# Identity products ahead of TensorE's waits in the last batch of a decoder layer's attention

## The reference

```
x = layernorm(x + ssm(x))                       # in_proj, causal conv, silu, selective scan
                                                #   (512 channels, 16 states, chunks of 64), gate, out_proj
x = layernorm(x + attention(x, ctx, ctx))       # 16 heads of 16, scores / 4, softmax, times v, w_o
x = layernorm(x + experts(x))                   # 8 experts by position, silu(x w1) * (x w3) w2, width 704
```

```
scores = einsum('bhqd,bhkd->bhqk', q, k) / sqrt(16)
attn   = softmax(scores, axis=-1)
out    = einsum('bhqk,bhkd->bhqd', attn, v)     # then heads side by side, times w_o, plus b_o
```

## Time and profile before

| | us |
|---|---|
| median of three runs | 2745.58 (2741.46 to 2746.72) |
| the profiled execution | 2741.8 |
| its span, first to last instruction | 2740.0 |
| TensorE (PE) busy | 2429.5 (89%) |
| VectorE (DVE) busy | 2123.5 (77%) |
| GpSimd (POOL) busy | 2073.6 (76%) |
| ScalarE (ACT) busy | 1821.1 (66%) |

### The profile page before, as it was taken

The page is one execution under the profiler, slowest core; times in us unless marked ns, Lnnn a source line. Parts: engine busy times, 40 slices in busy tenths (PEclk is TensorE's granted clock), DMA queues, the critical chain, the costliest instruction groups (busy, mean ns, idle before and its releaser), DMA issues. The chain is left out here.

```text
span 2740.0 us, 49530 instructions
## 1 busy us (share of the span) xinstructions
PE 2429.5 (89%) x14854; PEld 1667.0 (61%) x14854; DVE 2123.5 (77%) x3232; ACT 1821.1 (66%) x3972; POOL 2073.6 (76%) x999
## 2 busy tenths in 40 slices
PE   6678898989898898889999989988997879999997
PEld 5456666666666666666666666666665545555554
DVE  3788999999999999999999999999999722222333
ACT  3667888888888888888888887888887531111111
POOL 5999999999999999999999999999999400000000
PEclk9888999999999999999999999999998869999999
DMA  5355666666666666666666666666665342432221
GB/s 154 112 152 147 168 168 161 160 167 170 175 161 168 171 171 163 163 165 167 165 165 176 160 177 162 171 163 160 160 160 156 101 118 65 119 120 80 80 80 31
DMA packets 270168, 399.66 MB, mean 146 GB/s; under 512 B 115441, under 2 KB 190449, under 8 KB 265810
## 3 DMA queue, kind: packets, MB, share of 16 engines
q1 hardware_dynamic: 254546, 384.95, 52.9%
q10 hardware_dynamic: 15360, 11.55, 1.6%
HBM read 300.89 MB, written 94.37 MB: 144 GB/s over the span
## 5 line engine op out<-in xcount | busy, mean ns | idle before, releaser
L519 POOL TENSOR_TENSOR arena<-arena 128x1024 f32<-128x1024 f32 x512 | 1207.6, 2364 | 33.6 <-DMA arena<-w_dram 33.3
L623 ACT ACTIVATE dA_ps<-arena,a_neg 128x256 f32<-128x256 f32 x2048 | 880.1, 465 | 256.3 <-DVE arena L800 125.7
L800 DVE TENSOR_TENSOR_SCAN arena<-dA_ps,arena 128x512 f32<-128x512 f32 x672 | 802.7, 1207 | 75.5 <-ACT dA_ps L623 52.2
L529 POOL TENSOR_TENSOR arena<-arena 128x1024 f32<-128x1024 f32 (+1 forms) x416 | 808.4, 1943 | 18.0 <-DVE arena L800 15.0
L800 DVE TENSOR_TENSOR_SCAN dA_ps<-dA_ps,arena 128x512 f32<-128x512 f32 x352 | 415.7, 1204 | 3.8 <-POOL arena L519 3.4
L920 PE MATMUL a_ps<-xT,w_conv 128*128 128x256 f32 x1536 | 367.3, 389 | 0.0
L863 DVE TENSOR_REDUCE mx<-s_ps 128x2 f32<-128x512 f32 x497 | 333.4, 671 | 18.6 <-PE s_ps L920 18.6
L920 PEld LDWEIGHTS a_ps<-xT,w_conv 128*128 128x128 f32 x1536 | 286.5, 193 | 53.9 <-issue 16.3
L679 ACT ACTIVATE probs<-st_ps 128x512 f32<-128x512 f32 x493 | 285.2, 578 | 27.6 <-PE st_ps L920 25.4
L920 PE MATMUL s_ps<-k_st,q_st 96*128 96x256 f32 x994 | 262.2, 346 | 38.8 <-DVE mx L863 29.3
L920 PE MATMUL y_ps<-arena,sel 128*32 128x256 f32 x4096 | 258.5, 395 | 37.5 <-POOL arena L529 33.9
(11 more groups left out here) (117 smaller groups left out, 3275.4 us busy)
## 6 DMA issues: line engine op xcount, KB each, us to landing
arena<-delta_dram SPq DMA_DIRECT2D x512, 128.0 KB, 2.9
arena<-w_dram SPq DMA_DIRECT2D x512, 128.0 KB, 3.3
arena<-bc_dram SPq DMA_DIRECT2D x128, 256.0 KB, 4.5
q_st<-q_parts_dram SPq DMA_DIRECT2D x512, 64.0 KB
k_st<-k_parts_dram SPq DMA_DIRECT2D x512, 64.0 KB
w_dram<-u SPq DMA_DIRECT2D x32, 512.0 KB, 3.1
delta_dram<-delta SPq DMA_DIRECT2D x32, 512.0 KB, 3.9
k_parts_dram<-parts SPq DMA_DIRECT2D x32, 512.0 KB, 4.2
```

Source lines behind the costliest of these rows:

```text
L519: pool.tensor_tensor(dBu[:, n % NB], w_r[:, n // RP % 2, t % RP].unsqueeze(1).to_broadcast([P, QS, L]), bc_r[:, b.par, 0], ALU.mult).then_ ...
L529: pool.tensor_tensor(h[:, n % NH, states], h[:, n % NH, states], bc_r[:, b.par, 1, states], ALU.mult).then_inc(s_hC, 1)
L623: last = nc.scalar.activation(dA[n % NDA][:, q], delta_r[:, n // (2 * RP) % 2, t % RP], ACT.Exp, scale=a_neg[:, t, 2 * half + q:2 * half + ...
L800: nc.vector.tensor_tensor_scan(dst, decays, dBu[:, n % NB, 2 * half:2 * half + 2].rearrange("p q t -> p (q t)"), 0.0, ALU.mult, ALU.add).t ...
```

## The change

A helper `drain_products` issues `count` products ident x ident (128x128, f32) into a PSUM bank that is free at that point, and nothing for any batch but the last. It is called ahead of the waits in the pieces of the attention, and as pieces of their own (`idle`) before and behind transposes at the end. In `scores` and `scores_T` the wait for the stack and the wait for the rows of maxima move from the head of the piece to behind the products, so behind the wait for the bank; that holds for all batches. There are 158 products in all. The results are never read.

```diff
--- before.py
+++ after.py
@@ -923,6 +923,15 @@
                 for _ in range(count):
                     mm(s_ps[:, 0], g[:, 0, 0:P], g[:, 0], True, True)
 
+            def drain_products(b, count, out=None):
+                if b.c < B - 1:
+                    return
+                if out is None:
+                    bank_y.wait_read(pe)
+                    out = y_ps[:, 0:P]
+                for _ in range(count):
+                    mm(out, ident[:], ident[:], True, True)
+
             pe.wait_ge(s_zero, 1)
             idle_products(16)
             pe.wait_ge(s_const_v, N_BIAS)
@@ -1046,6 +1055,11 @@
                     bank_f.read_by(s_v, 1, b, 1)
                 return piece
 
+            def idle(count):
+                def piece(b):
+                    drain_products(b, count)
+                return piece
+
             def x_of(b):
                 return xt[:, b.c % NX]
 
@@ -1079,7 +1093,6 @@
             def scores(hd):
 
                 def piece(b):
-                    pe.wait_ge(s_stack[hd // HG], b.value(STACK_DMAS * 16, STACK_DMAS * 16))
                     n = b.value(H, hd)
                     if n:
                         pe.wait_ge(s_max, n - 1 if n > LATE_S + 1 else n)
@@ -1088,6 +1101,8 @@
                         for half in range(2):
                             pe.wait_ge(s_scan[half], NU * B)
                     out = scores_bank(n)
+                    drain_products(b, {0: 11}.get(hd, 0), out[:, 0, 0:P])
+                    pe.wait_ge(s_stack[hd // HG], b.value(STACK_DMAS * 16, STACK_DMAS * 16))
                     for tt in range(TT):
                         i = mm(out[:, tt], q_st[:, hd, tt * P:(tt + 1) * P], k_st[:, hd], True, True)
                     i.then_inc(s_s_mm, 1)
@@ -1095,6 +1110,7 @@
 
             def max_transpose(gr):
                 def piece(b):
+                    drain_products(b, 4 if gr < 2 else 0)
                     pe.wait_ge(s_max, b.value(H, HG * gr + HG))
                     bank_y.wait_read(pe)
                     nc.tensor.transpose(y_ps[0:HG * TT, L:],
@@ -1106,7 +1122,6 @@
             def scores_T(hd):
 
                 def piece(b):
-                    pe.wait_ge(s_m_row, b.value(NG * 16, 16 * (hd // HG) + 16))
                     n = b.value(H, hd)
                     if n:
                         pe.wait_ge(s_exp, n - 1 if n > LATE_ST + 1 else n)
@@ -1115,6 +1130,8 @@
                         for half in range(2):
                             pe.wait_ge(s_scan[half], NU * B)
                     out = scores_T_bank(n)
+                    drain_products(b, {4: 6, 8: 6, 12: 12}.get(hd, 0), out[:, 0, 0:P])
+                    pe.wait_ge(s_m_row, b.value(NG * 16, 16 * (hd // HG) + 16))
                     for kt in range(TT):
                         i = mm(out[:, kt], k_st[:, hd, kt * P:(kt + 1) * P], q_st[:, hd], True, True)
                     i.then_inc(s_st_mm, 1)
@@ -1123,6 +1140,7 @@
             def pv(gr):
 
                 def piece(b):
+                    drain_products(b, 5 if gr >= NG - 2 else 0)
                     pe.wait_ge(s_exp, b.value(H, HG * gr + HG))
                     pe.wait_ge(s_v, b.value(1, 1))
                     bank_f.wait_read(pe)
@@ -1137,6 +1155,9 @@
 
             def head_transpose(gr):
                 def piece(b):
+                    drain_products(b, (4, 22, 4, 5)[gr])
+                    if gr == 1 and b.c == B - 2:
+                        drain_products(b.ahead(1), 11)
                     pe.wait_ge(s_oT, b.value(NG, gr + 1))
                     bank_f.wait_read(pe)
                     for tt in range(TT):
@@ -1148,6 +1169,7 @@
 
             def attn_out(tt):
                 def piece(b):
+                    drain_products(b, 5 if tt == 0 else 0)
                     pe.wait_ge(s_onT, b.value(1, 1))
                     if tt == 0:
                         bank_a.wait_read(pe)
@@ -1172,9 +1194,12 @@
                 *[(O_OF, attn_out(tt)) for tt in range(TT)],
                 *[(O_OUT, out_proj(tt)) for tt in range(TT)],
                 *[(O_K, k_proj(m)) for m in range(KD)],
+                (O_ONT - 2, idle(4)),
                 (O_ONT - 2, transpose(lambda b: on, s_on, NG, s_onT_mm, s_onT, bank_a, a_ps)),
                 *[(O_Q, q_proj(m)) for m in range(KD)],
+                (O_X2T, idle(34)),
                 (O_X2T, transpose(x_of, s_x2, TT, s_x2T_mm, s_x2T, bank_a, a_ps)),
+                (O_X2T, idle(16)),
                 *[(O_ON + HG * gr, head_transpose(gr)) for gr in range(NG)],
                 (O_XP, x_proj),
                 *[(O_MT + HG * gr, max_transpose(gr)) for gr in range(NG)],
```

## The result

The changed kernel takes 2754.91 us (median of five runs, 2752.64 to 2758.85) against 2745.58 (median of five, 2741.46 to 2747.37): 1.0045 times as long, 95% interval 1.0033 to 1.0057. I had forecast 2746.5 us, within 0.2% of before; it is slower by more than that. The profiled execution takes 2757.5 us, span 2755.7, so 15.7 us more than the one of before. Between the means of the five runs it is 11.0 us: the profiled execution of before was a quick one, that of the changed kernel a slow one.

The account below looks back on a forecast made before the run. TensorE's gaps in the drain, and the low clock behind them, bound the kernel. A full clock gives 10.4 us, the products' overshoot takes it back: +2.6 us on a mean of 2743.9 makes 2746.5 us, range 2737 to 2757.

Parts of the forecast that it names:

- The mark: Experts' start: a warm first g_ps at 2259.4 us would equal the cold one at 2257.47, which loses 1.95 us.
- The page's dips: Granted clock on the profile page before: full nearly everywhere, dips in slices 32 and 33, the drain of the attention.
- The price of a product: TensorE, one f32 product of 128 columns: 0.24 us, range 0.21 to 0.32, from halving rows of 256 columns.
- The cheap rival: A product costs near the transposes' 0.07 to 0.13 us, so the whole 10.4 us is gained: 2733.5 us; chance 0.18.
- the dear one: Rival: 128-column streams do not hide their weight load, a product costs 0.32 us, +12.4 us: 2756.3 us; chance 0.20.
- The last 122 products and the work between: Drain from 2216.1 us to g_ps: 29.3 us of products plus work and waits, g_ps at 2262.0, +2.6 us.
- the cover: Products standing on TensorE's late waits, longer than these: 8.2 us on 4.25, 8.2 on 3.1 + 1.63, 3.8 on 2.67.
- The first 36 products: 2192 to 2216 us: later stack loads are won back by groups running warm, 0 us, range -1.5 to +1.5.
- The two waits stand in another order before the same matmul, which goes with the later one: 0: Moved waits in scores and scores_T, every earlier batch: the order of the waits changes nothing, 0 us.
- The clock: Sign: granted clock 1.00 from 2192 us through the experts' start; 0.50 anywhere in the stretch would show the forecast wrong.
- Slower by over 0.2%: Outcome for the whole kernel, slower by more than about 5.5 us: chance 0.27, against 0.52 same and 0.21 faster.

Follow-up runs that it names:

- e3: Changed kernel with 78 products instead of 158, both waits as before up to batch 30, no wait where a count is 0: 0.9972 of before, -7.9 us.
- e10: The kernel of e3 again, on another chip: 0.9982 of before, -4.5 us.
- e8: e3's 78 products, with both waits moved in all batches: 0.9994 of before, -1.0 us.
- e2: Changed kernel with its 158 products, but both waits as before up to batch 30: 1.0032 of before, +7.9 us.
- e4: e2 without the last 34 and 16 products: 1.0018 of before, +5.0 us.
- e1: Kernel before with only both waits moved in all batches, no products: 1.0026 of before, +6.8 us.
- e9: The kernel of e1 again, on another chip: 1.0021 of before, +6.7 us.
- e5: Kernel before with only the wait for the stack in scores moved, no products: 0.9996 of before, 0.0 us.
- e12: Kernel before with only the wait for the rows of maxima in scores_T moved, no products: 1.0015 of before, +5.6 us.

## Why the prediction was wrong, step by step

- **The mark** (start of g_ps plus 1.95 us for its cold start) was right: from the first g_ps on, the changed kernel needs 1.8 us less. The page's dips are slices 31 to 33, not 32 and 33.
- **The price of a product**, 0.24, was near: 0.223 in the longest group and 0.24 in those of five, and 122 of them 27.6 us instead of 29.3. The cheap rival (0.07 to 0.13) falls, and so does the dear one at 0.32: halving the two rows, 0.23 and 0.24, was the right way to a price that no row showed. The Trainium skill's rule (TensorE: Matmul & The Clock Gate, section Back-to-back issue gap) would have made it an estimate of 0.29. The trace disagrees: 0.223 / 2 = 0.11 an instruction is what half the columns of the earlier trace rows give, with no more for the load.
- **The last 122 products and the work between** were put at 16.65 + 29.3 = 45.95 us and took 45.2. The sum is closer than its parts: the products took 1.7 less, the work and waits between them 17.6, 0.95 more. That the cover is longer than the waits was right; e3, e10 and e8 show it from the other side.
- **The first 36 products** were put at 0, -1.5 to +1.5, and the stretch took 3.6 us more. It is again what stands above the waits: with 21 products in it, e3 goes from its max transpose at 2195.88 to 2219.32 in 23.4 us, as before (23.6), while e2, e4 and the changed kernel, with 36, take 27.2 to 27.4. It is not the first eleven: the first scores come 3.1 us behind the max transpose where it was 1.9, but behind the products TensorE still waits 0.36 us for the stack, and e1 and e9, without a product, have 3.1 and 3.0. (In e2 and e4 no wait is left behind the eleven; there it is 2.5.) At the heads' transpose the products stand above the wait; then TensorE waits for DMAs all the same: 0.97 us for the stack of head 8, 1.47 and 1.24 for the rows of heads 0 and 4, the last behind its six products. The groups between did not win it back. Which of the 36 products moved these DMAs no run shows. It is a term sized too small, by 3.6.
- **"The two waits stand in another order before the same matmul, which goes with the later one: 0"** is the step that failed. It was the one edit that works in all 32 batches, and it costs 6.7 +- 2.4 us (e9; 6.8 +- 2.6 in e1), about half of the loss. What I reasoned about, when this matmul may start, is not what costs: the pair of matmuls ends no later behind what it waits for (last section). What the runs show in its place is that ScalarE, VectorE and GpSimd wait longer in the batches, GpSimd by 6.5 us in all between the means of the table. How the order of two waits brings that about stays open.
- **The clock**: forecast 1.00 throughout, with 0.50 anywhere as a sign of being wrong; it was 0.50 for 6 us at 2220, behind waits of 0.97 and 1.47 us that have no products ahead of them. From 2228 us on it was right.
- In sum: +2.6 was forecast for the drain and +5.5 came, of which 3.6 are the first stretch; 0 for all else and about +6.7 came. Slower by over 0.2% had 0.27.

## What to carry to other kernels

Filler ahead of a wait must be shorter than the wait, counted at its own measured price: what it overshoots goes on the path, while what it falls short costs nothing as long as the clock stays up. Filler on a wait for a DMA can move the DMA too: the first stretch grew by 3.6 us although its products stood mostly on such waits. An edit made for one batch that moves an instruction in the loop's body is an edit of all batches: look at every engine-order line that changed, the waits' order too, or keep the old order where the filler isn't. And run the half with no filler in it as a control; here it held about half of the loss. Where one execution's marks move by 10 us from kernel to kernel with nothing changed ahead of them, two traces don't place a loss; the run times do.

## What the runs showed of the hardware that I had not expected

- Two waits of one matmul cost differently by their order in the program. Where the scores' matmul waits for VectorE's maximum, it starts 0.15 us behind the maximum's end before and in e2 (median of 21 cases each in the timelines from 300 to 1500 us), but only 0.05 us behind it in e1 (26 cases), with the wait for the maximum first. It goes with the order and the piece: in e5 it is 0.05 for the scores and 0.14 for scores^T (behind probs), in e12 0.14 and 0.05. The pair of matmuls ends 0.62 us behind the release before and 0.56 in e1. So with the late wait first the release itself is quicker, and the kernel is slower all the same.
- The clock came through gaps of 1 to 1.8 us in e3 with little loss (0.93 over 26 us), and was low behind e4's gap of 4.25 us (0.57 over 2265 to 2273). In the changed kernel it was 0.50 over 6 us behind gaps of 0.97 and 1.47 us, so the length of a gap alone does not tell.
